# Four units in twenty-four: which engine takes the relu of the attention scores out of PSUM

## What is computed

```
q = clip_round(q / s_q, -4, 3) * 16**-0.5;  k = clip_round(k, -4, 3);  v = clip_round(v, -4, 3)
attn = q @ k.T                                     # 12 heads of width 16, 196 x 196
attn = s_attn * round(clip(attn / 196 / s_attn, 0, 7))
out  = clip_round(attn @ v, -4, 3) @ Wproj.T + bproj
```

## Time and profile before

| | |
|---|---|
| median of the runs | 998.43 us |
| the profiled execution | 998.46 us, its span on the core 996.7 us |
| PE busy | 907.5 us (91%) |
| PEld busy | 785.2 us (79%) |
| DVE busy | 743.0 us (75%) |
| ACT busy | 702.9 us (71%) |
| POOL busy | 510.8 us (51%) |
| mean granted TensorE clock | 0.972 |

### The profile page before, as it was taken

The page is one execution under the profiler, slowest core; times in us unless marked ns, Lnnn a source line. Parts: engine busy times, 40 slices in busy tenths (PEclk is TensorE's granted clock), DMA queues, the critical chain, the costliest instruction groups (busy, mean ns, idle before and its releaser), DMA issues.

```text
span 996.7 us, 24830 instructions
## 1 busy us (share of the span) xinstructions
PE 907.5 (91%) x8170; PEld 785.2 (79%) x8170; DVE 743.0 (75%) x2855; ACT 702.9 (71%) x1516; POOL 510.8 (51%) x890
## 2 busy tenths in 40 slices
PE   5678999999999999998889899999999999999877
PEld 4566888888888888877677788888888888887766
DVE  4677878788788778777676777878878877878563
ACT  1367877777878777776566777777787877777652
POOL 4434564637465564636527456463746556463332
PEclk9797999999999999999999999999999999999889
DMA  7321121212121121212102112121202111000000
GB/s 228 105 64 34 49 64 41 61 45 74 32 69 49 53 65 41 61 45 68 44 25 73 32 53 65 41 64 42 77 29 69 50 53 49 10 13 13 14 13 28
DMA packets 31395, 52.52 MB, mean 53 GB/s; under 512 B 4653, under 2 KB 17949, under 8 KB 31269
## 3 DMA queue, kind: packets, MB, share of 16 engines
q1 hardware_dynamic: 31268, 50.94, 16.7%
HBM read 41.30 MB, written 9.63 MB: 51 GB/s over the span
## 4 chain that ended last, share of the span: by engine, by line
PE 34%; DVE 6%; ACT 6%; issue 5%; POOL 1%; DVEq 0%; ACTq 0%; POOLq 0%
PE mixed_ps L787 7%; PE near_ps L650 6%; PE mixed_ps L777 6%; PE mixed_ps L641 5%; PE scores_ps L708 2%; ACT relu L897 2%; PE near_ps L723 1%; PE turn_ps L663 1%; ACT hid L932 1%; ACT o_b L921 1%; DVE h L1222 1%; PE turn_ps L664 1%; PE mixed_ps L741 1%; DVE k_b L1182 1%; PE mixed_ps L742 1%
## 5 line engine op out<-in xcount | busy, mean ns | idle before, releaser
L897 ACT ACTIVATE relu<-scores_ps,c_prob 98x784 uint16<-98x784 f32 x384 | 348.8, 909 | 139.2 <-PE scores_ps L708 117.3
L650 PE MATMUL near_ps<-we,x_sb 128*128 128x192 f32 x1176 | 258.4, 341 | 12.5 <-DMA const_sb<-in_const 8.2
L978 POOL TENSOR_TENSOR ve<-mv,const_sb 128x1 f32<-128x1 f32 x294 | 60.3, 205 | 360.9 <-DVE mv L1319 357.1
L650 PEld LDWEIGHTS near_ps<-we,x_sb 128*128 128x128 f32 x1176 | 195.2, 196 | 19.1 <-DMA const_sb<-in_const 8.2
L991 POOL TENSOR_TENSOR expd<-econst,below 128x8 f32<-128x8 f32 x98 | 161.9, 1666 | 49.6 <-DVE below L1249 49.6
L981 POOL TENSOR_TENSOR rs<-ve,const_sb 128x1 f32<-128x1 f32 x294 | 173.9, 591 | 23.0
L1160 DVE TENSOR_SCALAR prob<-relu 98x784 bf16<-98x784 uint16 x384 | 151.1, 394 | 9.4 <-ACT relu L897 1.2
L787 PE MATMUL mixed_ps<-w_sb,hid 128*128 128x192 f32 x784 | 145.8, 330 | 0.0
L787 PEld LDWEIGHTS mixed_ps<-w_sb,hid 128*128 128x128 f32 x784 | 125.5, 191 | 1.4
L1135 DVE TENSOR_SCALAR xn<-h,mv,rs 128x192 f32<-128x192 f32 x196 | 74.1, 378 | 33.9 <-POOL rs L981 33.7
L932 ACT ACTIVATE hid<-mixed_ps,b_sb 128x384 f32<-128x384 f32 (+1 forms) x128 | 73.0, 586 | 36.2 <-PE mixed_ps L777 35.7
(11 more groups left out here) (155 smaller groups left out, 2208.2 us busy)
## 6 DMA issues: line engine op xcount, KB each, us to landing
x_sb<-in_x SPq DMA_DIRECT2D x98, 384.0 KB, 3.0
out<-out_sb SPq DMA_DIRECT2D x98, 96.0 KB, 1.6
we<-in_tok_w SPq DMA_DIRECT2D x1, 576.0 KB, 4.3
w_sb<-in_w SPq DMA_DIRECT2D x1, 384.0 KB
hid<-in_w_qkv SPq DMA_DIRECT2D x1, 288.0 KB, 5.5
hid<-in_w_qkv SPq DMA_DIRECT2D x2, 144.0 KB, 5.7
hid<-in_w SPq DMA_DIRECT2D x1, 256.0 KB
hid<-in_w SPq DMA_DIRECT2D x2, 128.0 KB
```

Source lines behind the costliest of these rows:

```text
L650: pe.matmul(dst, x_sb[:, tile % X_RING, j], we[:, j], start=j == 0, stop=False)
L897: act.activation(relu16[:, u % 2], scores_ps[0:KEYS, 2 * (u % VISIT):2 * (u % VISIT) + 2, 0:2 * SEQ], ACT.Relu, scale=c_prob[0:KEYS, :]).t ...
```

## The change

In the slots in which the heads of an image are evicted (2, 8, 14 and 20 of a pass), DVE makes the relu of the unit, as `tensor_scalar` with a multiplication and a maximum, out of PSUM. ACT leaves it out there. Each of the two engines has a semaphore of its own, and PE's `qk` waits for both. It makes 4 units of 24 in each group, 64 of 384 in all.

```diff
+        def on_vector(u):
+            return any((u - s) % SLOTS == 0 for s in AV)
+
+        def relus(g, units, vector):
+
+            return g.count(sum(on_vector(u) == vector for u in range(SLOTS)),
+                           sum(on_vector(u) == vector for u in range(units)))
...
-                wait(pe, act_relu, g.count(SLOTS, VISIT * v))
+                wait(pe, act_relu, relus(g, VISIT * v, False))
+                wait(pe, dve_relu, relus(g, VISIT * v, True))
...
             def relu(g, u):
+                if on_vector(u):
+                    return
                 act.wait_ge(qk_made, g.count(VISITS, u // VISIT + 1))
...
             def quantise(g, u):
 
                 wait(dve, av_made, g.count(GI, (u - RING) // PAIRS + 1))
-                dve.wait_ge(act_relu, g.count(SLOTS, u + 1))
+                if on_vector(u):
+                    dve.wait_ge(dve_relu, relus(g, u + 1, True))
+                else:
+                    dve.wait_ge(act_relu, relus(g, u + 1, False))
                 dve.tensor_scalar(prob[:, u % RING], relu16[:, u % 2], 7.0, None, ALU.min).then_inc(prob_out, 1)
+
+            def relu(g, u):
+                dve.wait_ge(qk_made, g.count(VISITS, u // VISIT + 1))
+                wait(dve, prob_out, g.count(SLOTS, u - 1))
+                dve.tensor_scalar(relu16[:, u % 2], scores_ps[0:KEYS, 2 * (u % VISIT):2 * (u % VISIT) + 2, 0:2 * SEQ],
+                                  c_prob[0:KEYS, :], 0.0, ALU.mult, ALU.max).then_inc(dve_relu, 1)
...
                     if two and s > 0:
                         quantise(two, s - 1)
+                    if two and inside and on_vector(s):
+                        relu(two, s)
                     for tile, st, mv, _, mv_sem in joined:
                         dve.bn_aggr(mv[:, tile % NT], st[:, tile % NT]).then_inc(mv_sem, 1)
```

More of the change, by code:

```diff
@@ L453, in vit_tower_kernel @@
         qk_made = sem("qk_made")
+        dve_relu = sem("dve_relu")
         act_relu = sem("act_relu")
```

## The result

The changed kernel takes 1013.22 us (median of 4 runs, 1012.16 to 1017.56), the kernel before 998.02 us (4 runs, 994.35 to 999.94). The ratio is 1.0163, with a 95% interval of 1.0132 to 1.0193: slower, by some 15 us. I had forecast slower, 1007.9 us in a range of 997 to 1015. The profiled execution took 1013.48 us, its span is 1011.7 us where it was 996.7.

A forecast was written before the change was run, and what follows sets the result against it. PE was taken to bound the kernel, busy 53.9 of each 56.0 us pass. Losses of 0.42 + 0.29 = 0.71 us, times twelve 8.5, plus 0.9 in group 7, gave 9.4 on 998.46: 1007.9 us, range 997 to 1015.

The forecast's parts named there:

- rival C: Late DVE is held a second time by POOL, at `k_b`: 0.42 us more a pass, 1012.9 us; chance 0.15.
- if the new waits stand elsewhere: Sign of being wrong: new PE waits not before `up` in slot 6 (0.4 us) and `down` in slot 23 (0.3 to 0.5).
- The bound, and what ACT gains: Repeating pass: PE sets the time, idle 2.1 of 56.0 us; ACT's relief gains 0.19 us at slot 22.
- The price of the relu: DVE's relu of 784 elements out of PSUM takes 0.97 us and pushes what follows by 0.90 us.
- Slot 2, "PE loses 0.42" in slot 6: DVE leaves slot 2 0.52 us late; `up` in slot 6 has 0.10 slack before `f_c`, so PE loses 0.42.
- Slot 20, "0.29": DVE leaves slot 20 0.59 us late; slot 23's `down` has 0.30 slack behind the residual, so PE loses 0.29.
- Slots 8 and 14 at nothing: Idle stretches of 0.70 and 0.66 us soon after absorb DVE's delay; 0.2 us is left, costed at nothing.
- Group 7, "the whole 0.9 us lands there": Group 7's pass, behind slot 14: DVE's chain is already exposed, so the relu's whole 0.9 us reaches PE.
- The sum: Twelve repeating passes at 0.71 us make 8.5, plus 0.9 in group 7: 9.4 us slower; other passes nothing.
- B: No change: about a quarter of the delay comes through and slot 22's gain pays for it; 998.5 us, chance 0.12.
- D: The whole relu is exposed in all 64 units: 57.6 us more, 1056 us; chance 0.03.
- A: Faster: DVE's lateness is absorbed before PE, only ACT's 0.19 us at slot 22 remains; 996.2 us, chance 0.14.

## Why the prediction was right, and where it was short

The direction and the kind of cost were right: DVE comes late to points at which PE needs it, and ACT's relief is too small to pay for that. The size was not: 9.4 us were forecast, 15 came. The time lies inside the range of 997 to 1015 us, but at the edge of the 1003 to 1013 that the forecast gave itself; the end at 1015 was there for rival C, whose second hold of `k_b` did not come. That is in part luck. By the prediction's own sign, "if the new waits stand elsewhere", its account of slot 2 was wrong.

- **The bound, and what ACT gains.** Right. PE's pass grew by PE's idle time, 0.9 us of the 1.2 in the first window; the other 0.3 stand as busy time, since at each new wait the record of the matmul ahead is no longer overlapped by the next. The heads are evicted 0.04 us behind the product as before; the wait at slot 22 fell to 0.74 us, forecast about 0.8. The run without any relu for these units puts the relief at 0.2 us a pass, forecast 0.19.
- **The price of the relu.** 1.026 us, forecast 0.97, from the widths' row; the whole and the half of it (1.026 and 0.62 us) give 0.41 us for 392 elements, 1.04 ns each, and 0.21 fixed.
- **Slot 2, "PE loses 0.42" in slot 6.** The term that failed. DVE came out of slot 2 about as late as said, 0.56 us (0.94 from the relu's start to the next one's, less the idle 0.38) for 0.52, but it met PE earlier than at `f_c`: at the projection in slot 3, which takes over the bank of `mixed_ps` that the choice's second step reads last. There was no slack there. My walk went "without a gap, through the choice of experts" and looked at PE only behind it. Nor was the 0.10 us at `up` slack: `up` begins 0.10 us after the end of `f_c` before the change and after it. The term measured 0.7 us, in four passes up to 1.1, in place of 0.42. At the projection PE is 0.73 and 1.08 us late: 0.56 from DVE's own lateness, the rest, 0.17 and 0.5, from POOL. The prediction gave POOL no part in slot 2; it let POOL's steps "move along with DVE" for slots 8 and 14 alone. In slot 2 they were moved into DVE's clips and slowed there, with the bias and the choice behind them. (Behind slots 8 and 14 one of POOL's two steps is slowed too, to 0.9 us in nearly every repeating pass, at next to no cost to PE.)
- **Slot 20, "0.29".** Right in place and kind, small in size: 0.35 with slot 20 alone. DVE's residual is 0.57 us late there, forecast 0.59. The 0.07 us that I allowed for the signal were too few: the down matmul begins 0.15 us after the residual's end wherever it waits for it, so the slack was 0.22 and not 0.30.
- **Slots 8 and 14 at nothing.** Right: 0.06 us a pass for both, though PE is 0.2 us late for a while behind slot 14.
- **Group 7, "the whole 0.9 us lands there".** Wrong. The wait after slot 14 is 1.51 us, as before. I had taken POOL's work to start "with the aggregation behind which the relu is now put". The relu stands ahead of that aggregation, and the normalisation there waits for an earlier one (at 488.44), which POOL took up late because it was busy with the powers (L1003) until then:

```profile
488.25 1.77 POOL L1003 TENSOR_TENSOR expd<-econst,below 128x8 f32<-128x8 f32 x1
...
489.79 1.03 DVE L1180 TENSOR_SCALAR relu<-scores_ps,c_prob 98x784 uint16<-98x784 f32 x1
...
490.00 0.19 POOL L990 TENSOR_TENSOR ve<-mv,const_sb 128x1 f32<-128x1 f32 x1
...
490.26 0.56 POOL L993 TENSOR_TENSOR rs<-ve,const_sb 128x1 f32<-128x1 f32 x1
...
490.86 0.38 DVE L1147 TENSOR_SCALAR xn<-h,mv,rs 128x192 f32<-128x192 f32 x1
...
492.16 0.44 PE L787 MATMUL mixed_ps<-f_hi,w_hi_a 128*128 128x384 f32 x1 [1.51 <-DVE h L1243]
```

  The relu ran in DVE's waiting time, and the 0.91 us that I read as exposed were its cover. The releaser of a wait doesn't tell what the releaser itself had waited for. That the pass is 0.8 us shorter goes with its granted clock, 0.98 where it was 0.95: PE's waits in it add up to 0.5 us more, its busy time to 1.1 less. Why the clock stood higher wasn't tried; over the traces of this case this pass takes 70.4 to 73.4 us.
- **The sum.** 12 x 0.71 + 0.9 = 9.4 was forecast. The change measured 15.9 in the twelve passes, -0.8 in group 7 and about nothing at the ends. Of the 7.4 us between 15.9 and 8.5 the slot-2 term makes 8 x (0.70 - 0.42) + 4 x (1.05 - 0.42) = 4.8, slots 20, 8 and 14 together 12 x 0.12 = 1.4; the remaining 0.1 us a pass shows only with all four slots together. The timelines say where it stands: behind slot 14, of whose delay mostly 0.06 to 0.2 us is left when PE has come to slot 22, and in groups 2, 3 and 9 at `up` in slot 6, which costs another 0.1 to 0.2 by waiting for `f_c`.
- **The rivals.** B's cancelling out and D's exposure of every relu did not come. A was the one that the change's idea stood for; its 0.19 us is real and too small. C had the right partner, POOL, at the wrong place: the clip `k_b` takes 0.80 us after the change as before (which of the two held the other there the rows don't say: `k_b` begins 0.09 us before `m`, and it is `k_b` that is long), and what the change adds is that POOL is slowed beside DVE: `rs`, of one element a row, takes 1.05 and 1.41 us beside the clips of slot 2, where it took 0.57. By the Trainium skill (SBUF — State Buffer, section "SBUF: two separate sides") whichever of the two starts first keeps the shared ports for its whole instruction, if DVE's is in a two-port mode. The trace of the change fits that for the clips and the quantisation of slots 2 and 3, for `rs` ends behind the last of them, by 0.40 us in the longer kind of pass; in which mode they run no row shows. It doesn't settle the relu: `ve` took 0.99 us beside one in slot 2 of the run with the aggregation first, and 0.19 beside one in slot 8 of the same run and in group 7 here.

## What to carry to other kernels

Moving work off an engine that the bottleneck waits for helps only where that work stands in the chain that it waits for. Look at what the very next instruction of the relieved engine waits for, before you count the moved time as won; here three of four were covered by PE's own product. When an engine becomes late, walk the bottleneck's instructions one by one from that point, hand-overs of buffers included, and take the first that has less slack than the delay; the last of a dense run isn't the one that counts. A row without a wait is not a row with slack: count from the end of what the instruction needs to its start, and compare that with the same distance where it does wait (0.15 us in both cases here). Include the third engine whose small operations move along with the late one. A small operation that can be put off behind the awaited one can be worth as much as four large ones taken away.

## What the runs showed of the hardware

A POOL operation on one element a row can take two to four times its time when DVE is dense beside it: `rs` 0.57 us before, 1.05 and 1.41 after; `ve` 0.24 before, 0.99 in the run with the aggregation first. Which of DVE's operations does it stays open, and so does the part of a relu out of PSUM: `ve` beside one took 0.99 us in one slot and 0.19 in another. In the repeating passes PE's matmul began 0.15 us after the end of the DVE operation that it waited for at the projection and at `down`, and 0.10 us after it at `up`, with the change and in the experiments alike. And one run of the kernel with slot 2 alone had a granted clock of 0.95 in all its repeating passes, with 54.5 us of PE's busy time where the same kernel's other run had 54.1 at 1.00; the order of instructions was the same; that is 0.4 us of a pass, more than half of what slot 2 alone costs.
